# Flamingo block with a mixture of experts: products of ones ahead of the first group, GpSimd's power moved, the expert rows loaded by one burst

## The reference

```python
x = x + tanh(g_xattn) * attention(layernorm(x), ctx, mask, Wq, Wkv)   # softmax over 128 keys, 16 heads of 16
h = layernorm(x)
top_logits, top_idx = top_k(h @ w_router, 2);  scores = softmax(top_logits)
moe    = sum over the 2 choices of scores * (silu(h @ fc1_a[e]) * (h @ fc1_b[e])) @ fc2[e]
shared = (silu(h @ gate_w) * (h @ up_w)) @ down_w
x = x + tanh(g_ffn) * (moe + shared)
```

## Time and profile before

| | |
|---|---|
| median of 3 runs | 360.67 us (360.33 to 360.98) |
| the profiled execution's own time | 361.57 us |
| its span, first to last instruction | 359.5 us |
| mean granted TensorE clock | 0.961 |
| busy: PE, PEld, DVE, ACT, POOL | 312.0, 253.1, 255.8, 170.8, 121.2 us |

### The profile page before, as it was taken

The page is one execution under the profiler, slowest core; times in us unless marked ns, Lnnn a source line. Parts: engine busy times, 40 slices in busy tenths (PEclk is TensorE's granted clock), DMA queues, the critical chain, the costliest instruction groups (busy, mean ns, idle before and its releaser), DMA issues.

```text
span 359.5 us, 7932 instructions
## 1 busy us (share of the span) xinstructions
PE 312.0 (87%) x2404; PEld 253.1 (70%) x2404; DVE 255.8 (71%) x780; ACT 170.8 (48%) x325; POOL 121.2 (34%) x133
## 2 busy tenths in 40 slices
PE   1948879888888895775996999999999999999994
PEld 1836767677767684654443758898888888988884
DVE  5367569698989898883799763767676767644786
ACT  2344757665757464544566051644444444433231
POOL 4541111216161616055162016383434343432000
PEclk9998999999999987888898999999999999999999
DMA  8676585866475546211025200233333232211683
GB/s 229 212 207 195 156 236 146 206 181 189 148 200 165 166 138 188 92 62 59 2 74 162 60 2 16 73 97 99 103 98 99 90 104 90 86 42 27 264 289 121
DMA packets 34916, 46.50 MB, mean 129 GB/s; under 512 B 5599, under 2 KB 29539, under 8 KB 34370
## 3 DMA queue, kind: packets, MB, share of 16 engines
q1 hardware_dynamic: 28002, 28.77, 28.6%
q10 hardware_dynamic: 3424, 8.72, 7.7%
q0 software_dynamic: 3456, 8.56, 7.1%
HBM read 21.55 MB, written 12.62 MB: 95 GB/s over the span
## 4 chain that ended last, share of the span: by engine, by line
PE 57%; SPq 12%; DVE 10%; DMA 8%; issue 4%; ACT 4%; another core or an unknown queue 2%; POOL 1%; ACTq 1%; DVEq 0%; POOLq 0%
PE ps L1589 31%; SPq L352 7%; DMA stacks<-work 6%; SPq L359 4%; PE ps L1275 3%; PE ps L1476 2%; DVE mx L893 2%; PE ps L1639 2%; PE ps L1561 2%; PE ps L1340 2%; PE ps L1373 2%; PE ps L1389 2%; PE ps L1581 2%; ACT probs L623 2%
## 5 line engine op out<-in xcount | busy, mean ns | idle before, releaser
L541 POOL DMA_INDIRECT expert_rows<-v_s,slot_u x39 | 38.4, 984 | 61.9 <-ACT v_s L806 49.2
L893 DVE TENSOR_REDUCE mx<-ps 128x8 f32<-128x1024 f32 x32 | 39.1, 1223 | 12.5 <-PE ps L1340 11.8
L503 POOL TENSOR_TENSOR work<-work 128x512 bf16<-128x512 f32 x16 | 18.6, 1162 | 66.0 <-ACT work L592 66.0
L623 ACT ACTIVATE probs<-ps 128x1024 f32<-128x1024 f32 x32 | 32.6, 1019 | 15.5 <-PE ps L1373 8.5
L1193 DVE TENSOR_TENSOR act<-ps,sil 128x256 f32<-128x256 f32 x39 | 16.6, 425 | 29.9 <-ACT sil L799 21.7
L1589 PE MATMUL ps<-fc_hi,xs_hi 128*128 x78 | 34.2, 438 | 0.0
L799 ACT ACTIVATE sil<-ps 128x256 f32<-128x256 f32 x39 | 15.0, 385 | 39.3 <-PE ps L1589 38.2
L1340 PE MATMUL ps<-stacks 96*128 96x128 bf16 x256 | 21.3, 230 | 12.5 <-DVE mx L893 6.4
L1589 PE MATMUL ps<-fc_lo,xs_hi 128*128 x78 | 30.9, 396 | 0.0
L1589 PE MATMUL ps<-fc_hi,xs_lo 128*128 x78 | 30.8, 394 | 0.0
L1340 PEld LDWEIGHTS ps<-stacks 96*128 96x128 bf16 x256 | 16.9, 104 | 17.3 <-DVE mx L893 8.9
(11 more groups left out here) (207 smaller groups left out, 818.3 us busy)
## 6 DMA issues: line engine op xcount, KB each, us to landing
stacks<-work SPq DMA_DIRECT2D x93, 128.0 KB, 2.7
xs_in<-dispatched SPq DMA_DIRECT2D x39, 129.0 KB
fc_s<-in_fc ACTq DMA_DIRECT2D x8, 512.0 KB, 3.6
stacks<-expert_rows SPq DMA_DIRECT2D x4, 1024.0 KB, 6.0
fc_s<-in_fc ACTq DMA_DIRECT2D x8, 256.0 KB, 4.0
ctx_s<-in_ctx_t SPq DMA_DIRECT2D x8, 192.0 KB
x_all<-in_x SPq DMA_DIRECT2D x1, 1536.0 KB, 8.9
out<-x_all SPq DMA_DIRECT2D x3, 512.0 KB, 6.2
```

What stands on the lines that cost most here:

```text
L503: nc.gpsimd.tensor_tensor(out[:, 2, :], rest, out[:, 1, :], ALU.subtract).then_inc(ready, 1)
L541: nc.gpsimd.indirect_dma_start(ys, bass.IndirectOffsetOnAxis(dst_u[:, r:r + 1], 0), y_out[:, r, :], None, bounds_check=2 * T - 1, oob_is_e ...
L623: nc.scalar.activation(probs[:, 2 * j + h], ps_t, ACT.Exp, scale=HD ** -0.5).then_inc(probs_ok[j][h], 1)
L893: nc.vector.reduce_max(mx[:, j, 8 * h:8 * h + 8], ps_s, AX_X).then_inc(max_ok[j][h], 1)
```

## The change

- PE issues 56 bf16 products of a 128x128 tile of ones with itself before the product of the gates (the first in the program before), and 24 behind it. Their result is overwritten.
- ACT's `second(0)` for the queries stands ahead of the three DMA issues of the first piece, no longer behind them.
- GpSimd's `power2(G - 1, 0)` stands inside `dispatch(G - 3)`, behind the first of its four scatters.
- VectorE: `gated(2)` stands ahead of `table`; `low_of_fc1(0)` to `(2)` move behind `gated(3)`.
- Tail: four buffers for the expert rows (two more, in `probs`), all four loads issued at once, the adds in eight single steps at other places among the products, the last chunk's adds ahead of its last product. The four last stores are issued by SP and ACT in turn.

```diff
+        p_f = probs[:, :, :, :].rearrange("p a h t -> p (a h t)")
+        y_in = [home[:, 8 * D * r:8 * D * (r + 1)].rearrange("p (t k d) -> p t k d", t=CH, k=2)
+                for home in (q_f, p_f) for r in range(2)]
...
             for c in range(NCH):
-                if c >= 2:
-                    sp.wait_ge(y_added, c - 1)
-                sp.dma_start(y_in[c % 2], y_view[:, CH * c:CH * c + CH]).then_inc(y_got[c % 2], 16)
-                if c < 2:
-                    continue
-                sp.wait_ge(y_added, c - 1)
-                sp.dma_start(out_view[:, CH * (c - 2):CH * (c - 1), :],
-                             x_all[:, CH * (c - 2):CH * (c - 1), :]).then_inc(out_done, 16)
-            sp.wait_ge(y_added, NCH - 1)
-            sp.dma_start(out_view[:, B - 2 * CH:B - CH, :], x_all[:, B - 2 * CH:B - CH, :]).then_inc(out_done, 16)
-            for t in range(CH):
+                sp.dma_start(y_in[c], y_view[:, CH * c:CH * c + CH]).then_inc(y_got[c], 16)
+            for c in range(NCH - 1):
+                sp.wait_ge(y_added, c + 1)
+                sp.wait_ge(base_ok, CH * (c + 1))
+                sp.dma_start(out_view[:, CH * c:CH * c + CH, :], x_all[:, CH * c:CH * c + CH, :]).then_inc(out_done, 16)
+            for t in range(0, CH, 2):
...
                 for m in range(4):
+                    if g == G - 3 and m == 1:
+                        power2(G - 1, 0)
                     nc.gpsimd.indirect_dma_start(
...
             first(0, q_done, qst, q_pc, q_ok[0], ps_q0)
+            second(0, qr_ok, q_rest, q_pc, q_ok[1])
             sa.wait_ge(q_ok[0], 1)
...
-            low_of_fc1(0)
             gated(1)
             places(g)
             weights(g)
+            gated(2)
             table()
-            gated(2)
-            low_of_fc1(1)
-            low_of_fc1(2)
             gated(3)
             relink()
-            low_of_fc1(3)
-            low_of_fc1(4)
+            for e in range(5):
+                low_of_fc1(e)
             times(1, 0)
...
+            def add_expert(c, k):
+                xc = x_all[:, CH * c:CH * c + CH, :]
+                if k == 0:
+                    ve.wait_ge(y_got[c], 16)
+                    if c < 2:
+                        ve.wait_ge(base_ok, CH * (c + 1))
+                else:
+                    ve.wait_ge(y_half, c + 1)
+                nc.vector.tensor_tensor(xc, xc, y_in[c][:, :, k], ALU.add).then_inc(y_added if k else y_half, 1)
 
             for j in range(NJ):
+                if j == NJ - 1:
+                    add_expert(0, 0)
                 product(2, j)
                 low_of_hidden(2, j)
-            add_experts(0)
+            add_expert(0, 1)
+            add_expert(1, 0)
+            add_expert(1, 1)
             product(3, 0)
-            add_experts(1)
+            add_expert(2, 0)
+            add_expert(2, 1)
+            ve.wait_ge(y_added, 3)
             sum_and_add(2, 2 * CH, sums)
             low_of_hidden(3, 0)
             product(3, 1)
             low_of_hidden(3, 1)
             product(3, 2)
-            add_experts(2)
+            add_expert(3, 0)
             low_of_hidden(3, 2)
+            add_expert(3, 1)
             product(3, 3)
             low_of_hidden(3, 3)
-            add_experts(3)
...
+            pe.wait_ge(cum_ok, 1)
+            def warm(count):
+                for n in range(count):
+                    nc.tensor.matmul(ps[:, 0, 0:P], ones_b[:, :], ones_b[:, :], start=True, stop=True)
+            warm(56)
             pe.wait_ge(small_in, 32)
             pe.wait_ge(const_ok, 11)
             nc.tensor.matmul(ps_c[:, 0:2], ones_r[:, :], gate_r[:, :], start=True, stop=True).then_inc(gates_done, 1)
+            warm(24)
```

More of the change, by code:

```diff
@@ L293, in build_program @@
         ysc = [S[f"ysc{r}"] for r in range(4)]
-        y_got = [S["y_in0"], S["y_in1"]]
+        y_got, y_half = [S[f"y_in{c}"] for c in range(4)], S["y_half"]
         xst_done, xst_ok, h_done, silm_ok, act_ok = (S["xst_done"], S["xst_ok"], S["h_done"], S["silm_ok"],
@@ L673, in _ @@
                                  q_pc[:, p, :]).then_inc(qst[0], 16)
-            second(0, qr_ok, q_rest, q_pc, q_ok[1])
             values_in(0)
@@ L834, in _ @@
                     nc.scalar.activation(hid_hi[:, j, :], sil_sh[:, j % 2], ACT.Copy).then_inc(hhi_ok, 1)
+            for t in range(1, CH, 2):
+                sa.wait_ge(base_ok, B - CH + t + 1)
+                sa.dma_start(out_view[:, B - CH + t, :], x_all[:, B - CH + t, :]).then_inc(out_done, 16)
         @block.vector
```

9 lines of the change are left out of this document (1 added, 8 removed).

## The result

The changed kernel takes 346.44 us (median of 4 runs, 345.56 to 347.26); the kernel before takes 360.5 (4 runs). The ratio is 0.9654, 95% interval 0.9612 to 0.9696, so 14 us faster where I forecast 5.5. A second measurement, in another session, gave 0.9644 (0.9588 to 0.9700), so the result stands. A ratio counts the executions within 1.5% of their kernel's fastest, a median all of them.

What follows compares the result with a forecast made beforehand. PE was taken to bound the kernel, with 57% of the chain that ended last. From 360.67 us, start -1.9, gated products -2.2, clock -1.3 and tail -0.1 (power 0) gave 355.2 us, range 353.4 to 358.3.

Steps and rivals of the forecast that it cites:

- Term: 0: GpSimd's power moved inside the last block's scatters: no gain, from -0.3 to +0.3 us.
- I carry the 1.9 through whole: Start: the 1.9 us gained at the first maximum reaches the end undiminished, +-0.6 for the clock.
- follows by semaphores and moves with it: Attention behind the first maximum at 25.06: no outside load has a fixed time, so all moves with the start's 1.9 us.
- The cover that I named: End of attention: VectorE's next `attended` waits for PE until 170.41, so running the power earlier gains 0.
- -3.5: Before the experts: gated products -2.2 us, and the clock behind them counted at -1.3.
- the 1.7: At `down_0`: the clock stays up after PE's shorter wait, -1.7 us in the profiled execution, 1.3 counted in the forecast.
- -0.1: Tail: adds no longer ahead of the final sums give 1.8 us, the order ahead takes 1.7.
- the stores by two queues: End of the tail: each store is 0.45 us of issue and the last landing ends the run as now, 0.
- Rival B: Tail gains too, PE not being held: 1.8 us in place of 0.1, 353.5 us; chance 0.08.
- C: Tail: four loads share the DMA engines and land together at 342.8, costing 7.7 us, 362.9 us; chance 0.05.
- D: No change: start's gain lost at a fixed attention point, VectorE's backlog cancels the gated gain, 360 us; 0.10 with small mixtures.
- A: Clock at `keys(0)`, `down_0` or elsewhere gives less than counted: loses 1.3 to 3.2 us, 356.5 to 358.4; chance 0.22.

Runs made afterwards that it cites:

- b1_start: Kernel before with the start's two edits alone (56 and 24 products of ones, second(0) ahead of three DMA issues): ratio 0.9875, median 357.93 us.
- a1_nostart: Changed kernel without the start's two edits (no products of ones, second(0) behind the DMA issues): ratio to before 0.9748.
- a5_noones: Changed kernel without the products of ones, second(0) still ahead of the three DMA issues: ratio to before 0.9780.
- c2_fill40: Changed kernel with 40 more products of ones between the first two score products of group 0: ratio to before 0.9707.
- x2_after_waits96: Changed kernel with 96 satisfied waits on PE between the first two score products of group 0: ratio to before 0.9754.
- a0_all: The changed kernel once more, unaltered, beside three kernels that each leave one edit out: ratio to before 0.9625.
- b4_tail: Kernel before with the tail's edit alone (four loads at once, eight single adds, stores by two queues): ratio 0.9963.
- a2_nopower: Changed kernel with GpSimd's power of the last block behind all four scatters, as before: ratio to before 0.9755.
- b2_power: Kernel before with one edit, GpSimd's power of the last block's first half behind the first scatter instead of all four: ratio 0.9907.
- b3_gated: Kernel before with one edit, gated(1) to gated(3) ahead of the table and the low halves: ratio 0.9861.
- c1_tail: Changed kernel with another order of VectorE's tail adds, chunk 2's last product ahead of the first add: ratio to before 0.9578.
- c4_fill64_tail: Changed kernel with 64 more products of ones in group 0's gaps and another order of the tail's adds: 342.82 us, ratio to before 0.9604.
- x1_waits160: Kernel before with 160 satisfied waits on PE ahead of the gates' product: ratio 1.0068.

## Why the prediction was wrong

Two steps failed. For certain it is "Term: 0" for GpSimd's power: it gives 3.3 to 4.7 us. Probably it is also "I carry the 1.9 through whole" at the start, which comes out at 4.4 to 5.6 by the ratios. The gated products came out larger than their term, but not clear of the noise, and the tail had two errors that nearly cancel.

**The start: the mechanism right, "I carry the 1.9 through whole" probably wrong.** The 2.1 us at the first maximum is what the chain gave. The start as a whole came out at 4.5 (`b1_start`) and 4.4 (`a1_nostart`), the products of ones in `a5_noones` at 4.5 to 5.6 against the changed kernel's three ratios of other sessions. Each has 3 to 4 us of uncertainty, so that each alone would allow 1.9. What I had not thought of is group 2, 16.0 to 16.4 in the changed kernel in place of 17.5 to 21.4. I had written that all of the attention "follows by semaphores and moves with it"; but PE's instruction stream got 160 instructions longer, so its fetches fall elsewhere, and one of them no longer meets the weight load on whose heels the key stacks go. `c2_fill40` brought the collision back by 80 instructions that delay nothing, with the long issue (1.42 us for 0.45), the slow load (7.4 us for 5.3) and ACT's wait (3.66 for 1.43). That is good evidence for this chain in group 2, from one profiled execution and read after the fact; what it is worth in the kernel's time is not shown, since other groups lengthen by as much without it, and one execution (`x2_after_waits96`) has the slow load, 7.5 us, with neither a fetch nor a long group. The size of the load may have its part: where a later group's 0.75 MB met a fetch (second issue 1.08 to 1.44 us, eleven times outside of the session of `a0_all`), the next group took 16.4 to 17.4 us, no longer than its neighbours. No run tests it. Why a fetch of 16 KB slows 1.25 MB by 2 us is not shown.

The Trainium skill, "TensorE: Matmul & The Clock Gate", Part 1, holds the ramp for not worth fitting, under 1% of a span. The trace agrees on the size: by the clock the products of ones give 2.1 of 360 us, 0.6%. But they last to the end, and the edit as a whole came out at more.

**GpSimd's power: "Term: 0" wrong, it gives 3.3 to 4.7.** The cover that I named, `attended` waiting for PE until 170.41, belonged to that execution. There ACT's last copy of the attention came late:

```profile
168.61 0.60 ACT L632 ACTIVATE ot_s<-ps 128x512 f32<-128x512 f32 x1 [4.68 <-remote]
```

In `b4_tail`, with the same program there, PE was ready first and VectorE stood for the power, as in six of the eight profiled executions without the edit. The two others (before, `a2_nopower`) are among the five in which ACT was late in every group, see the last section. Behind the power PE waited 3.21 us in `b4_tail`, and the clock fell from 172.3 to 175.7; in `b2_power` PE waited 0.93 us there and it stayed up. That the wait decides it is not shown: in `b3_gated` PE waited 3.20 and the clock stayed up too. A wait by which I had hidden a term at nothing had to be checked for what it is itself made of. In the trace the power is worth 2.3 us behind the attention (11.6 for 9.3), a late PE hides part of it (10.7 in the kernel before); the rest of the 3.3 to 4.7 is not traced.

**The gated products and the clock: right in the profile, -3.5 against 5.0 to 5.9 measured.** Of the profile the forecast steps came to the tenth (7.9 us from the third tanh, PE's wait, a clock of 1.00); `down_0` took 7.17 us in place of 8.68, 1.5 of the 1.7. All 8 profiled executions without this edit have a clock at 0.50 at `down_0`, none of the 12 with it. The measured sizes are larger, but 3.5 lies within the interval of either. This edit and the power fill the same stretch, so neither has one worth: it takes 42.5 to 44.2 us with neither, 38.5 to 40.5 with one, 35.8 to 38.3 with both.

**The tail: right in PE's wait, two sizes wrong that nearly cancel.** PE was held for 1.57 (1.4 forecast). Up to the final sums it is +0.4 in the trace for -0.1, and the stores by two queues, which I had put at 0, come with 0.6 less behind them: -0.2 in all, near the forecast by luck. Alone it measured 0.9963, an interval that holds 0. Rival B's 1.8 was there to be had: `c1_tail` and `c4_fill64_tail` took 1.7.

**The rivals.** C did not happen: the first add began at 319.69, the forecast landing was 335.1 - 15.8 = 319.3 (15.8 is the shift of the last scatter), so the other three loads cost the first one at most 0.4 us. D's fixed point does not exist, and A's loss came nowhere. None of them had the attention's inner course in it, so the range, made of them, was too narrow. So were the 0.2% that I took for the least change a measurement can tell: the intervals are 0.4 to 1.1% each way.

## What to carry to other kernels

Instructions added to one engine move its instruction fetches, and a fetch can meet a large load on which a later stage waits: after an edit compare the periods of stages that it doesn't touch. A cover read from one execution holds only if what makes it late is there in the others too; profile a second one before a term is put at zero. Fill an engine's idle gaps in front of work that runs at the clock's lower level. Before adds are put ahead of an operation, count what waits for that operation to free its buffer. And count in the trace the instructions that an edit really added: waits had been put together in pairs.

## What had not been expected of the hardware

- An instruction on PE that holds two satisfied waits cost 0.106 us (80 in a row, from 1.2 to 9.9 us, in `x1_waits160`).
- A fetch of 16 KB beginning 0.3 to 0.6 us ahead of a DMA issue of ACT made that issue take 1.04 to 1.42 us for 0.45, for group 2 7 times of 7 (for later groups 0.69 to 1.32).
- With the four last stores issued by SP and ACT in turn it took 5.6 us from the start of the final sums to the end (13 profiled executions), with SP alone 6.2 (7). No run changes the stores alone.
- In 5 of 20 profiled executions (the kernel before among them, and all four of one session) ACT's exponentials came 1 to 2 us late in every group from the third on, with a wait that the profile puts down to "remote"; the trace's semaphore events there come in steps of 0.7 us (33 to 44 gaps of over 0.55 us up to the end of the attention, 6 to 19 in the other executions; 4820 to 4896 events in all in place of 5954 to 6002), and groups 3 to 5 mostly last 17.7 to 18.8 us in place of mostly 16.4 to 17.6. The medians of before were 363.9 in that session and 358.5 to 360.5 in the others. What makes it is not settled. Ratios within a session were alike, 0.9625 and 0.9644.
